# Row loads held six tiles behind the tensor engine, idle rows one tile at a time, and no memset behind the scatters of a routed expert kernel

## The reference, cut to what matters

```python
x = x + gnn(layernorm(x), adj)              # adj @ x, W1, rmsnorm, silu, W2
h = layernorm(x)
xn = (h - mean) * rsqrt(var + 1e-5) * gamma + beta
logits = xn @ Wr + br                       # 8 experts
top_vals, top_idx = top_k(logits, 2)
w = softmax(top_vals)
y = 0
for e in range(8):
    hid = gelu(xn @ W1[e] + b1[e])          # 128 -> 256
    y = y + (hid @ W2[e] + b2[e]) * w_full[..., e, None]
x = x + y
```

## Time and profile before

| | before |
|---|---|
| median of 3 runs | 447.06 us (445.47 to 447.8) |
| the profiled execution | 446.49 us |
| its span, first to last instruction | 444.7 us |
| mean granted TensorE clock | 0.985 of full |
| busy in the span: PE / DVE / ACT / POOL | 402.4 / 298.2 / 281.7 / 298.1 us |
| DMA, mean over the span | 120 GB/s, 53.51 MB in 41175 packets |
| scatters of results, scatters of rows | 92 of 979 ns, 64 of 1061 ns |
| memsets of `leave_space` | 105 of 380 ns |
| row loads, blocks of idle rows | 92 and 28, 132.5 KB each |

### The profile page before, as it was taken

One profiled execution on the slowest core, in us unless ns is written; L12 is line 12 of the kernel. 1 busy time (PEld: TensorE's weight loads), 2 busy tenths in 40 slices (PEclk: granted clock), 3 DMA queues, 4 the chain that ended last, 5 costly groups with the idle time before them and its releaser, 6 DMA issues.

```text
span 444.7 us, 11925 instructions
## 1 busy us (share of the span) xinstructions
PE 402.4 (90%) x2932; PEld 349.0 (78%) x2932; DVE 298.2 (67%) x1267; ACT 281.7 (63%) x652; POOL 298.1 (67%) x445
## 2 busy tenths in 40 slices
PE   0899999999999999998879986799999899999993
PEld 0567777777777878776779875699989898999993
DVE  4597877889887888967744561266566666755652
ACT  1278776777677778777785543366676776545540
POOL 1233568787777888887781678766656566777775
PEclk9999999999999999999999999689999999999998
DMA  6879873233332231111165155455555453331110
GB/s 181 257 228 313 295 215 105 65 99 107 110 119 78 81 110 39 50 49 40 61 177 133 57 132 152 139 138 146 135 150 148 123 135 104 102 98 37 36 38 31
DMA packets 41175, 53.51 MB, mean 120 GB/s; under 512 B 5842, under 2 KB 35794, under 8 KB 40468
## 3 DMA queue, kind: packets, MB, share of 16 engines
q1 hardware_dynamic: 33040, 32.95, 27.3%
q0 software_dynamic: 6096, 18.52, 11.8%
q10 hardware_dynamic: 1972, 1.28, 1.1%
HBM read 38.01 MB, written 22.31 MB: 136 GB/s over the span
## 4 chain that ended last, share of the span: by engine, by line
PE 64%; DVE 11%; issue 11%; DVEq 7%; DMA 2%; ACT 1%; another core or an unknown queue 1%; POOL 1%; ACTq 0%; POOLq 0%
PE banks L810 12%; PE banks L793 11%; PE banks L627 10%; PE banks L650 10%; PE banks L615 6%; PE banks L636 5%; PE banks L672 3%; DVEq L1504 2%; DVEq L1525 2%; PE banks L773 2%; PE banks L662 2%; DVE result L1532 1%; DVEq L1532 1%; DVE hidden L1082 1%; DVEq L1518 1%
## 5 line engine op out<-in xcount | busy, mean ns | idle before, releaser
L561 POOL DMA_INDIRECT out<-result,rows_in x92 | 90.1, 979 | 54.0 <-DVE result L1532 48.6
L810 PE MATMUL banks<-w_sb,hidden_e 128*128 (+1 forms) x736 | 105.5, 285 | 6.1 <-DVE result L1532 4.8
L810 PEld LDWEIGHTS banks<-w_sb,hidden_e 128*128 128x128 f32 x736 | 93.5, 195 | 9.2 <-issue 8.5
L946 ACT ACTIVATE hidden_e<-banks 128x512 f32<-128x512 f32 x92 | 54.9, 597 | 49.5 <-PE banks L793 39.3
L505 POOL DMA_INDIRECT rows_dram<-rows_out,row_of x64 | 67.9, 1061 | 23.4 <-issue 10.8
L627 PE MATMUL banks<-gw_sb,agg 128*128 128x512 f32 x128 | 67.3, 611 | 0.9 <-DVE gw_sb L983 0.9
L650 PE MATMUL banks<-gw_sb,hidden_t 128*128 128x128 f32 x512 | 67.6, 275 | 0.0
L650 PEld LDWEIGHTS banks<-gw_sb,hidden_t 128*128 128x128 f32 x512 | 63.5, 192 | 0.8
L858 ACT ACTIVATE hidden<-banks 128x512 f32<-128x512 f32 x64 | 38.2, 597 | 30.4 <-PE banks L627 27.3
L636 PEld LDWEIGHTS banks<-fixed,hidden 128*128 128x128 f32 x256 | 30.5, 141 | 34.4 <-issue 29.7
L940 ACT ACTIVATE xg_t<-banks,ones 128x128 f32<-128x128 f32 x92 | 33.5, 364 | 33.1 <-PE banks L773 19.9
(11 more groups left out here) (147 smaller groups left out, 765.0 us busy)
## 6 DMA issues: line engine op xcount, KB each, us to landing
rows_in<-rows_dram SPq DMA_DIRECT2D x92, 132.5 KB
adj<-adj_t SPq DMA_DIRECT2D x16, 512.0 KB, 4.9
x_tok<-x SPq DMA_DIRECT2D x16, 256.0 KB, 4.0
rows_dram<-idle_in POOLq DMA_DIRECT2D x1, 3710.0 KB
rows_dram<-idle_in SPq DMA_DIRECT2D x28, 132.5 KB
out<-result,rows_in POOLq DMA_INDIRECT x92
w_sb<-w SPq DMA_DIRECT2D x1, 1024.0 KB, 6.3
b_bc<-b SPq DMA_DIRECT2D x1, 1024.0 KB, 10.7
```

The lines of the kernel that those rows point to most:

```text
L561: nc.gpsimd.indirect_dma_start(out=out, out_offset=bass.IndirectOffsetOnAxis(ap=rows_in[:, i % RING][:, IDX_AT:IDX_AT + 1].bitcast(U32), a ...
L810: last = pe.matmul(y_ps(i)[:, w], hidden_e[:, i % 4, w * HCE + c], w2_sb[:, bass.ds(at + c * D, D)], start=(c == 0 and i >= EARLY), stop=( ...
L946: nc.scalar.activation(hidden_e[:, i % 4], h_ps(i), ACT.Gelu).then_inc(gelu_done, 1)
```

## The change

Four things are edited.

- `load_rows(i)` waits from tile 6 on until tile i - 6 has been turned (`LEAD`), besides the wait that it had.
- The blocks of idle rows were six ahead of tile 20's load and then one behind every second load. Now there is one behind each load from tile 20 to tile 47.
- GpSimd's `send` no longer clears anything where no weight copy follows. The `leave_space` in the loop of the first stage stays: 13 of the 105 memsets are left.
- TensorE turns the columns of the second table at (15, 2), behind the narrow matmuls of tile 11, instead of ahead of them at (15, 1). On ScalarE step 3 is reordered: copy of the turned tile 3, the first two normalising activations, the weight copies of tile 3, gelu of tile 1; before, the activations stood at the end of step 2, and the weight copies of tile 3 ahead of its tile copy. The other steps keep their order; their code is only cut into functions.

```diff
--- before.py
+++ after.py
@@ -56,6 +56,8 @@
 
 WIDE_LAG, NARROW_LAG, SUM_LAG = 2, 4, 4
 AHEAD = 8
+
+LEAD = 6
 PER_WORD = 4
 
 SPACE = 320
@@ -416,6 +418,8 @@
                     start = sp.value_load(first_row[0:1, i:i + 1], min_val=0, max_val=IDLE + (NC - 1) * P)
                 else:
                     start = sp.value_load(left_row[0:1, i - NT:i - NT + 1], min_val=0, max_val=IDLE + (NC - 1) * P)
+                if i >= LEAD:
+                    sp.wait_ge(xt_turned, i - LEAD + 1)
                 if i >= RING:
                     sp.wait_ge(result_sent[(i - RING) % SENDS], 16 * ((i - RING) // SENDS + 1))
                 sp.dma_start(rows_in[:, i % RING], rows_dram[bass.ds(start, P), :]).then_inc(rows_here[i % RING], 16)
@@ -431,17 +435,14 @@
                 load_rows(i)
 
             sp.wait_ge(ends_ready, 1)
-            fills = iter(range(NC))
-            for c in range(6):
-                fill_end(next(fills))
             sp.wait_ge(table_ready, 3)
             sp.wait_ge(idle_sent, 16)
             for k, n in enumerate(sent_before(NG - 1)):
                 sp.wait_ge(rows_sent[k], 16 * TPG * n)
             for i in range(EARLY, NT):
                 load_rows(i)
-                if i % 2 and (c := next(fills, None)) is not None:
-                    fill_end(c)
+                if i - EARLY < NC:
+                    fill_end(i - EARLY)
             sp.wait_ge(fill_sent, 16 * NC)
             for i in range(NT, TILES):
                 load_rows(i)
@@ -570,9 +571,7 @@
                     send_result(n)
                 else:
                     send_rows(what, n)
-                if then is None:
-                    leave_space()
-                else:
+                if then is not None:
                     place_high(then)
 
             a, z = NG - 2, NG - 1
@@ -762,7 +761,7 @@
                     router(NG - 1)
                 elif at == (11, 1):
                     rank_pairs(NG - 1)
-                elif at == (15, 1):
+                elif at == (15, 2):
                     turn_columns(1)
 
             def tile_step(step):
@@ -921,37 +920,46 @@
 
             words = {}
 
-            def tile_step(step):
-                if (i := tile_at(step, 0)) is not None:
-                    if i >= 4:
-                        act.wait_ge(h_done, i - 3)
-                    if i < NT:
-                        if i % PER_WORD == 0:
-                            words[i // PER_WORD % 2] = act.value_load(word[0:1, i // PER_WORD:i // PER_WORD + 1],
-                                                                      min_val=0, max_val=2 ** 24 - 1)
-                        at = expert(words, i, HE, True)
-                        nc.scalar.activation(w1_low[:, i % 4], w1_sb[:, bass.ds(at, HE)], ACT.Copy
-                                             ).then_inc(low_placed, 1)
-                        if not high_by_gpsimd(i):
-                            at = expert(words, i, HE, False)
-                            nc.scalar.activation(w1_high[:, i % 4], w1_sb[:, bass.ds(at, HE)], ACT.Copy
-                                                 ).then_inc(high_placed, 1)
-                    act.wait_ge(xt_turned, i + 1)
-                    nc.scalar.activation(xg_t[:, i % 4], xt_ps(i), ACT.Identity, bias=ones[:, 0:1]
-                                         ).then_inc(xg_t_ready, 1)
-                if (i := tile_at(step, WIDE_LAG)) is not None:
-                    if i >= 4:
-                        act.wait_ge(y_done, i - 3)
-                    act.wait_ge(h_done, i + 1)
-                    nc.scalar.activation(hidden_e[:, i % 4], h_ps(i), ACT.Gelu).then_inc(gelu_done, 1)
+            def place_weights(i):
+                if i >= 4:
+                    act.wait_ge(h_done, i - 3)
+                if i < NT:
+                    if i % PER_WORD == 0:
+                        words[i // PER_WORD % 2] = act.value_load(word[0:1, i // PER_WORD:i // PER_WORD + 1],
+                                                                  min_val=0, max_val=2 ** 24 - 1)
+                    at = expert(words, i, HE, True)
+                    nc.scalar.activation(w1_low[:, i % 4], w1_sb[:, bass.ds(at, HE)], ACT.Copy
+                                         ).then_inc(low_placed, 1)
+                    if not high_by_gpsimd(i):
+                        at = expert(words, i, HE, False)
+                        nc.scalar.activation(w1_high[:, i % 4], w1_sb[:, bass.ds(at, HE)], ACT.Copy
+                                             ).then_inc(high_placed, 1)
+
+            def keep_rows(i):
+                act.wait_ge(xt_turned, i + 1)
+                nc.scalar.activation(xg_t[:, i % 4], xt_ps(i), ACT.Identity, bias=ones[:, 0:1]
+                                     ).then_inc(xg_t_ready, 1)
+
+            def gelu(i):
+                if i >= 4:
+                    act.wait_ge(y_done, i - 3)
+                act.wait_ge(h_done, i + 1)
+                nc.scalar.activation(hidden_e[:, i % 4], h_ps(i), ACT.Gelu).then_inc(gelu_done, 1)
 
             act.wait_ge(table_ready, 2)
             for step in range(TILES + WIDE_LAG):
                 if step == EARLY:
                     act.wait_ge(table_ready, 4)
-                tile_step(step)
-                if step == 2:
+                now, before_now = tile_at(step, 0), tile_at(step, WIDE_LAG)
+                if step == 3:
+                    keep_rows(now)
                     normalise2(NG - 1, (0, 1))
+                    place_weights(now)
+                elif now is not None:
+                    place_weights(now)
+                    keep_rows(now)
+                if before_now is not None:
+                    gelu(before_now)
                 if step == 3:
                     normalise2(NG - 1, (2, 3))
                 if step == 5:
```

## The result

The changed kernel takes 453.97 us (median, 453.14 to 455.18) where the kernel before took 446.99 us in the same series: a ratio of 1.0164 [1.0133, 1.0195]. It is 7 us slower; the forecast was 5 us faster. The profiled execution has a span of 452.1 us against 444.7, so the 7.4 us to be explained lie inside the span.

A forecast was written before the change was run, and what follows sets the result against it. TensorE, carrying 64% of the span, was taken as the bound. 446.49 - 0.75 - 1.6 - 0.8 - 2.0 = 441.3 us for the profiled execution, 441.9 as a median; range 435.0 to 449.5.

The forecast's parts named there:

- Part 4: SyncE, tiles 20 to 47: one block per load makes 2.40 us a tile; 2 to 3 us lead left, nothing lost.
- Part 3: GpSimd without memsets behind results: worth nothing in steady state, gain 0.8 us at the end.
- Part 5: Tiles 17 to 23, where 13.2 us are lost: sooner scatters and changed row loads win back 2.0 us.
- Part 1: ScalarE step 3, tile copy first: TensorE turns tile 4 at 229.6, tile 5 at about 232.7; gain 0.75 us.
- Part 2: TensorE's column turn one place later: tile 11's matmuls fill its idle, gain 1.6 us; load 20 about 1.8 us earlier.
- slow stretch: TensorE's turns from tile 17 to 24: 28.00 us for 7 tiles, completions arriving late, 13.2 us lost.
- Rival E: Scatters without a pause hold up TensorE's completions, ten more in the fourth stretch at 0.88 us each: 452.7 us; chance 0.13.
- fourth stretch: The 34 steps after the slow stretch, 72.50 us, 2.13 a tile; GpSimd waits for VectorE there nearly always.
- rival D: SyncE's lead is eaten by over 2.40 us a tile; decides from 2.56, 447.2 us at 2.8; chance 0.12.
- rival B: Late completions in the slow stretch stay as they are: 443.9 us; chance 0.22.

The follow-up runs named there:

- e4: The kernel before with only GpSimd's memsets behind results and rows taken away: 452.69 us, 1.0103.
- e7: The kernel before with only ScalarE's new order in step 3 and the column turn one place later: 446.65 us, 0.9945.
- e5: The kernel before with the memset behind results 1 to 29 twice as wide (640 instead of 320 elements): 442.21 us, 0.9846.
- e9: The kernel before with ScalarE's new order, the later column turn, 640-element memsets behind results up to 79 and none behind 86 to 91: 429.38 us, 0.9576.
- e15: The changed kernel with e9's memsets, without SyncE's wait for the tile six ahead; one block to each load stays: 437.46 us, 0.9781.
- e10: The changed kernel with e9's memsets; SyncE's wait for the tile six ahead and one block to each load stay: 440.48 us, 0.9822.
- e16: The changed kernel with e9's memsets and the idle-row blocks sent as before; the wait for the tile six ahead stays: 429.03 us, 0.9591.
- e1: The changed kernel with GpSimd's memsets behind row scatters and results put back: 447.39 us, 0.9981.
- e8: The kernel before with results 2 to 19 written by plain DMAs to a place of their own, their output rows left out: 434.88 us, 0.9675.
- e3: The changed kernel with idle-row blocks sent as before (six ahead of load 20, then one to every second load); the wait stays: 449.78 us, 1.0018.

## Why the prediction was wrong, step by step

Two steps failed. Part 4 put SyncE's blocks at nothing, out of a lead of 12.8 us; the lead was 6.4 us at tile 26, and tiles 31 to 47 took 6.6 us longer than before. Parts 3 and 5 took the missing memset for a gain of 2.8 us; alone it costs 1.0% (e4), and in the changed kernel it is also what took SyncE's lead.

**Part 1, right.** Forecast: tile 4 at 229.6, tile 5 at 232.7. In e7 they stand at 229.78 and 232.96. In the changed kernel itself the gain is covered by the 1.6 us lost at tile 1 (tile 4 at 232.3).

**Part 2, right in size, wrong in its second half.** The idle ahead of the column turn is 0.49 us (forecast: under 0.8), the first table copy at 261.73 (forecast: about 262). Parts 1 and 2 together bring 2.2 us by tile 17 in e7's trace, for 2.35 forecast. But load 20 went out at 265.50, 0.2 us earlier and not 1.8. SyncE's last wait for the row scatters (L440) ends at 264.30 in e7, 2.6 us behind that copy. I had named this condition, that the last rows have landed, and then costed it at nothing.

**Part 3, wrong outside the end.** At the end the last scatters are 1.27 us apart, not the 1.12 of the forecast, because GpSimd idles 0.30 us between two scatters and 0.17 behind a memset; the gain was 0.5 us, not 0.8. In the backlog, too, it was 1.27 us and not 1.13. The step that failed is the one that found the memset "worth nothing" in steady state and looked no further: three scatters at 221 to 225, which no part priced, cost 1.6 us.

**Part 5, wrong.** The trace of before had shown the right suspect (packed scatters, completions late), but I let the loss shrink with the time in which scatters are packed, 17 us instead of 23. It goes by how closely they are packed, from 1.51 us on: with more room the slow stretch vanishes (e5, e9). With less it stays what it was. It took 29.7 us, not 23 to 27, within what kernels with the memset take. The 13.2 us of the earlier trace rows were real and could be had, with the opposite edit. e4 prices parts 3 and 5 together at +1.0%, where the forecast had 2.8 us the other way; most of that loss (3.2 us by tile 8) lies ahead of the stretch, and no part priced anything there.

**Part 4, costed at 0.** Two terms were mis-sized. SyncE needs 2.55 us a tile, not 2.40 (e15: from 264.2 to 333.1 for 27 tiles); part 4 itself goes over from 2.40 to 2.45 without giving a reason. And the lead of 12.8 us at tile 26, from which 2 to 3 us were to be left, did not exist: tile 26's load went out 6.4 us ahead of its turn (292.5, 298.9), because SyncE had been held up as well. Nor is it there when nothing holds SyncE up. In e10 and e15 it is 2.7 and 2.4 us at tile 26: the load of tile 20 goes at 264.6 and 264.3, once the last rows have landed, and a TensorE that isn't held up turns tile 20 only 5 us later. The 20.3 us of the kernel before were lead only because TensorE stood still. A sign that SyncE, too, can be slowed in that stretch stood in the earlier trace rows, where a load pair with its block took 5.24 us; I used it for rival D's condition and not for the lead. Nor did the wait for the tile six places ahead matter: it was the blocks (e15, e16).

**The rivals.** Rival E's mechanism (a pause was what kept completions flowing) is what e1, e4, e5 and e9 show, and its 452.7 us is near the 453.97 measured. But its place was wrong: the extra scatters of the fourth stretch did no harm that the trace shows. Its price agrees only by luck, because rival D came true as well. D decided from 2.56 us a tile with a full lead; with the lead cut to 7 us, 2.55 was enough, and TensorE waited for loads at tiles 34, 36 to 39 and 45 to 48; D had named tiles 35 to 50. I had treated D and E as alternatives, at 0.12 and 0.13; they were one event, since what E does to SyncE starts D. B's sign, a slow stretch of about its old length, did come, but not its 443.9 us, since B left out the start and SyncE. The Trainium skill (SBUF — State Buffer, Who interferes with whom) says that DMA never contends with a compute engine for SBUF. No run contradicts this: the plain DMAs of e8, at 166 GB/s, did no harm. But it says nothing of the pace of scatters, and rival B read it as if this pace could change nothing; e5 and e9 show that it does.

## What to carry to other kernels

An instruction that computes nothing between two DMAs can be the most valuable one on its engine; before taking it away, make it longer once and see which way the time goes. Where a trace shows completions arriving late on several engines at once, look at how closely the scatters of GpSimd follow each other, and spread them: here 0.27 us more between them was worth over 3% (e7 to e9). And a lead in time is a stock: compare the issuing engine's own pace with the consumer's, and ask what could take the stock away just before it is needed.

## What the runs showed of the hardware

- While GpSimd's scatters follow each other every 1.27 us, a tile is copied up to 10 us after TensorE's record of its turn (tile 18 of the changed kernel; 14.4 us for tile 19 of e3), and many of SyncE's instructions take 0.70 us instead of 0.04 to 0.3. At 1.51 us the copies are as late (10.2 us for tile 21 of e7), but in the kernel before SyncE is hardly slower. At 1.78 us with the old order of blocks (e9) no tile from 17 on is copied more than 2 us late. What the engines share there, and why it ends near 1.78 us, no run shows; it stays open.
- The loss comes later the nearer the spacing is to 1.78 us: at 1.27 and 1.51 it begins at tile 18 or 19, at 1.65 most of it lies at tiles 29 to 34, at 1.75 at tiles 32 to 38. That would fit something that fills up slowly, which is argued and not shown.
- A scatter of 128 rows holds GpSimd for 0.97 us, one of 64 rows for 0.91, a plain DMA of 64 KB for 0.55.
